# Second attention of a two-layer block: queries and output projection from rounded parts, fills dealt anew

## What is computed

```python
x = x + tanh(g_ffn[0]) * L0_ffn(...)                    # its sum is taken up in the second attention
x = x + tanh(g_xattn[1]) * L1_xattn(layernorm(x), ctx_768, ...)
x = x + tanh(g_ffn[1]) * L1_ffn(layernorm(x), ...)

def L1_xattn(x, y):                     # 16 heads of 32, 120 keys to a batch
    q = (x @ wq + bq).reshape(B, SQ, 16, 32)
    k = (y @ wk + bk).reshape(B, SKV, 16, 32)
    v = (y @ wv + bv).reshape(B, SKV, 16, 32)
    attn = softmax(einsum('bqhd,bkhd->bhqk', q, k) / sqrt(32))
    return einsum('bhqk,bkhd->bqhd', attn, v).reshape(B, SQ, 512) @ wo + bo
```

## Time and profile before

| | |
|---|---|
| median of 3 runs | 3941.38 us (3939.68 to 3944.68) |
| the profiled execution | 3940.56 us |
| its span in the trace | 3938.5 us |
| busy over the span | PE 94%, PEld 74%, DVE 74%, ACT 48%, POOL 28% |
| the second attention in the trace | about 2033 to 2557 us |
| the second mixture of experts | from there to the end, with TensorE's matmuls on nearly the whole chain that ended last |

### The profile page before, as it was taken

One profiled execution on the slowest core, in us unless ns is written; L12 is line 12 of the kernel. 1 busy time (PEld: TensorE's weight loads), 2 busy tenths in 40 slices (PEclk: granted clock), 3 DMA queues, 4 the chain that ended last, 5 costly groups with the idle time before them and its releaser, 6 DMA issues. The chain is left out here.

```text
span 3938.5 us, 62704 instructions
## 1 busy us (share of the span) xinstructions
PE 3699.6 (94%) x21884; PEld 2925.5 (74%) x21884; DVE 2924.7 (74%) x4545; ACT 1903.8 (48%) x2703; POOL 1098.4 (28%) x1008
## 2 busy tenths in 40 slices
PE   7899999999899999999979999849999999999998
PEld 4556665566468889889965555549999999999997
DVE  5567766676658788787737888578888788888885
ACT  2555555556445555554425445314444444444443
POOL 2222211222001111111026565313333434333332
PEclk9999999999899999999989999959999999999999
DMA  4010010100248787776640221126877777776874
GB/s 161 29 32 13 29 34 31 32 11 20 81 160 277 245 284 248 263 272 204 205 158 34 74 93 54 49 87 206 238 235 234 229 217 238 237 238 208 237 234 128
DMA packets 386958, 596.53 MB, mean 151 GB/s; under 512 B 26559, under 2 KB 192511, under 8 KB 386559
## 3 DMA queue, kind: packets, MB, share of 16 engines
q1 hardware_dynamic: 352575, 521.68, 39.7%
q0 software_dynamic: 24864, 58.54, 6.8%
q10 hardware_dynamic: 9368, 14.33, 1.0%
HBM read 535.36 MB, written 59.12 MB: 151 GB/s over the span
## 5 line engine op out<-in xcount | busy, mean ns | idle before, releaser
L1282 DVE TENSOR_TENSOR e_all<-e_all_raw,e_WH 128x2048 fp32r<-128x2048 f32 x240 | 545.5, 2289 | 36.5 <-ACT e_WH L1276 22.9
L1441 PE MATMUL bank<-e_xh,e_WH 128*128 128x256 f32 x1984 | 563.6, 284 | 9.5 <-issue 9.5
L1441 PE MATMUL bank<-e_xh,e_all 128*128 128x256 f32 x1984 | 562.5, 284 | 0.0
L1441 PE MATMUL bank<-e_xl,e_WH 128*128 128x256 f32 x1984 | 562.5, 284 | 0.0
L1276 ACT ACTIVATE e_WH<-e_all_raw 128x2048 fp32r<-128x2048 f32 x240 | 458.3, 1910 | 189.0 <-DMA e_all_raw<-in_w 188.8
L1494 PE MATMUL bank<-e_WH,e_hh 128*128 128x512 f32 x1192 | 473.7, 397 | 0.0
L1494 PE MATMUL bank<-e_WH,e_hl 128*128 128x512 f32 x1192 | 468.3, 393 | 0.0
L1441 PEld LDWEIGHTS bank<-e_xh,e_WH 128*128 128x128 f32 x1984 | 379.4, 191 | 14.7 <-issue 13.7
L1441 PEld LDWEIGHTS bank<-e_xl,e_WH 128*128 128x128 f32 x1984 | 379.4, 191 | 0.9
L1441 PEld LDWEIGHTS bank<-e_xh,e_all 128*128 128x128 f32 x1984 | 379.4, 191 | 0.0
L1517 ACT ACTIVATE e_sil<-bank 128x256 f32<-128x256 f32 x248 | 95.2, 384 | 367.0 <-PE bank L1441 362.3
(11 more groups left out here) (380 smaller groups left out, 9242.6 us busy)
## 6 DMA issues: line engine op xcount, KB each, us to landing
e_all_raw<-in_w SPq DMA_DIRECT2D x320, 512.0 KB, 5.0
f_wl_raw<-in_w SPq DMA_DIRECT2D x120, 1024.0 KB, 6.3
e_all_raw<-in_w SPq DMA_DIRECT2D x80, 1024.0 KB
e_rest_raw<-in_w SPq DMA_DIRECT2D x72, 1024.0 KB, 5.5
f_X<-in_x SPq DMA_DIRECT2D x32, 256.0 KB, 2.7
f_R<-in_x SPq DMA_DIRECT2D x32, 256.0 KB, 4.3
x<-f_R SPq DMA_DIRECT2D x32, 256.0 KB, 2.0
a_X<-x SPq DMA_DIRECT2D x32, 256.0 KB, 4.8
```

Source lines behind the costliest of these rows:

```text
L1282: dve.tensor_tensor(self.WL(p), self.raw(p), self.WH(p).bitcast(F32), ALU.subtract).then_inc(self.w_ready.sem, 1)
L1441: mm = nc.tensor.matmul(up[n % RING][:, q * ROWS:q * ROWS + ROWS], w, xx[:, c, :], start=(c == 0 and i == 0), stop=(c == DC - 1 and i == 2))
```

## The change

It computes `q` and `o` from rounded parts. Each operand is split in a high part (rounded to `fp32r`, a form of float32 whose matmuls show as one record each) and a low part (the rest, rounded too); a product is then high x high, high x low and low x high, so twelve matmuls stand in the place of eight records. ScalarE writes the high parts of `yt` and `pv`, and VectorE then reads the same PSUM bank again and writes the low parts (`low`): eight more VectorE operations to a batch, and the bank is free only after them. The weights are split once, ScalarE rounding and VectorE subtracting (`weights_high`, `weights_low`).

`o` is no longer emptied by ScalarE. VectorE reads it from PSUM in `result`, gates it and adds the residual in one instruction. Keys and values are loaded for one batch at a time, the keys by DMA straight into `kcur`, so that ScalarE copies none. The fills are dealt anew: both `pv` that were done in step 7 are now done in steps 0 and 1 of the next body, `yt` stands beside `o` in steps 3 to 6, and two fills of `q` stand in step 7.

```diff
-FILLS1 = ((("q", 2), ("nt", 3), ("r", 2)),
-          (("q", 3), ("yt", 0), ("r", 3)),
-          (("pv", 2), ("yt", 1), ("pv", 3), ("yt", 2)),
-          (("yt", 3), ("o", 0), ("q", 0)),
-          (("o", 1),),
-          (("o", 2), ("nt", 0)),
-          (("o", 3), ("nt", 1), ("r", 0)),
-          (("q", 1), ("pv", 0), ("pv", 1), ("nt", 2), ("r", 1)))
+FILLS1 = ((("q", 2), ("r", 1), ("pv", 0), ("nt", 3)),
+          (("pv", 1), ("r", 2)),
+          (("pv", 2), ("q", 3), ("pv", 3), ("r", 3)),
+          (("o", 0), ("yt", 0)),
+          (("o", 1), ("yt", 1)),
+          (("nt", 0), ("o", 2), ("yt", 2)),
+          (("nt", 1), ("o", 3), ("yt", 3)),
+          (("q", 0), ("r", 0), ("q", 1), ("nt", 2)))
...
-NORM1_AT = {3: (2, 0), 4: (2, 1), 1: (1, 2), 2: (1, 3)}
+NORM1_AT = {4: (2, 0), 5: (2, 1), 2: (1, 2), 3: (1, 3)}
...
+                def load_kv(i):
+                    if i >= 2:
+                        sp.wait_ge(s_done, STEPS1 * (i - 1))
+                    for r in range(4):
+                        p = slice(DH1 * r, DH1 * r + DH1)
+                        sp.dma_start(kcur[p, i % 2, :, r % 2, :], k.kT1[p, :, ORDER[i] * CL:ORDER[i] * CL + CL]).then_inc(k_in[i % 2], 16)
+                    if i >= 2:
+                        wait_filled(sp, i - 2, ("pv", 3))
+                    sp.dma_start(V[:, i % 2, :], k.V1[:, ORDER[i], :]).then_inc(v_in[i % 2], 16)
...
                     elif kind == "q":
-                        pe.wait_ge(wq_in, 32)
+                        pe.wait_ge(w_ready, 1)
...
-                            mm = nc.tensor.matmul(m, wq[:, c, a * P:a * P + P], xT[:, c, :], start=(c == 0), stop=(c == DC - 1))
+                            wh, wl = (by_rows(w)[:, c, a * P:a * P + P] for w in (wqh, wql))
+                            for j, (w, x) in enumerate(((wh, xTh), (wh, xTl), (wl, xTh))):
+                                mm = nc.tensor.matmul(m, w, x[:, c, :], start=(c == 0 and j == 0), stop=(c == DC - 1 and j == 2))
...
+                def weights_high(to, raw, there):
+                    act.wait_ge(*there)
+                    act.activation(to[:, :], raw[:, :], ACT.Copy).then_inc(w_high, 1)
...
+                weights_high(wqh, wq_raw, (wq_in, 48))
                 for n in bodies:
+                    if n == 0:
+                        weights_high(woh, wo_raw, (wo_in, 48))
...
+                    bk_, c_ = fill(i, f)
+                    dve.wait_ge(filled[bk_], c_)
+                    dve.wait_ge(r_biased, a)
+                    dve.scalar_tensor_tensor(x, mb[bk_], k.gate[:, 1:2], x, ALU.mult, ALU.add).then_inc(emptied[bk_], 1)
                     wait_emptied(dve, i, f)
-                    dve.wait_ge(r_biased, a)
-                    dve.tensor_tensor(x, x, gated[:, t % 2, :], ALU.add).then_inc(x3_ready, 1)
-                    dve.wait_ge(x3_ready, a)
                     dve.bn_stats(bst3[:, t, :], x).then_inc(bn3_step, 1)
...
+                def low(n, f):
...
+                    dve.wait_ge(kept_high, high(i, f))
+                    if kind == "yt":
+                        part = slice(a * P, a * P + P)
+                        x = dve.tensor_tensor(xTl[:, :, part], chunks(mb[bk_]), xTh[:, :, part].bitcast(F32), ALU.subtract)
+                    else:
+                        x = dve.scalar_tensor_tensor(OTl[:, a, :], mb[bk_], bv[:, a:a + 1], OTh[:, a, :].bitcast(F32),
+                                                     ALU.add, ALU.subtract)
+                    x.then_inc(emptied[bk_], 1)
...
+                weights_low(wql, wq_raw, wqh, 1)
                 for n in bodies:
                     for s in range(STEPS1):
                         u = STEPS1 * n + s
+                        if n == 0 and s == 0:
+                            weights_low(wol, wo_raw, woh, 2)
                         if softmax(n):
                             centre(u)
+                        low(n, FILLS1[s][0])
...
                             total(u)
-                        for f in FILLS1[s]:
+                        for j, f in enumerate(FILLS1[s]):
+                            if j:
+                                low(n, f)
```

More of the change, by code:

```diff
@@ L1696, in attention1 @@
         chunks = lambda bk_: bk_.rearrange("p (c n) -> p c n", c=DC)
-        wq_in, wo_in, kv_in, bf_in, folded, kzeroed = \
-            sem("wq_in"), sem("wo_in"), sem("kv_in"), sem("bf_in"), sem("folded"), sem("kzeroed")
-        k_ready = sem("k_ready")
+        wq_in, wo_in, bf_in, folded, kzeroed = sem("wq_in"), sem("wo_in"), sem("bf_in"), sem("folded"), sem("kzeroed")
+        k_in, v_in = [sem(f"k_in{i}") for i in range(2)], [sem(f"v_in{i}") for i in range(2)]
+        w_high, w_ready, kept_high = sem("w_high"), sem("w_ready"), sem("kept_high")
         x_in = [[sem(f"x_in{r}{t}") for t in range(QT)] for r in range(2)]
@@ L1738, in turned_in, with high @@
             return u if 0 <= u < STEPS1 * B else None
+        def high(i, f):
+            n = len(SPLIT1) * (i + LATE.get(f, 1) + 2) + SPLIT1.index(f)
+            return sum(1 for m in range(n + 1) if there(m // len(SPLIT1) - 2, SPLIT1[m % len(SPLIT1)]))
         comb = lambda i: i >= PLAIN
@@ L1900, in do @@
                         for c in range(DC):
-                            mm = nc.tensor.transpose(m[:, c * P:c * P + P], Y[:, a, c * P:c * P + P], k.ident[:, :])
+                            mm = nc.tensor.transpose(m[:, c * P:c * P + P], Y[:, (QT * i + a) % YRING, c * P:c * P + P], k.ident[:, :])
                     elif kind == "q":
-                        pe.wait_ge(wq_in, 32)
+                        pe.wait_ge(w_ready, 1)
                         for t in range(QT):
@@ L1917, in do @@
                         for c in range(DC):
-                            mm = nc.tensor.matmul(m, OT[:, c, a * P:a * P + P], wo[:, c, :], start=(c == 0), stop=(c == DC - 1))
+                            oh, ol = (o[:, c, a * P:a * P + P] for o in (OTh, OTl))
+                            for j, (o, w) in enumerate(((oh, woh), (oh, wol), (ol, woh))):
+                                mm = nc.tensor.matmul(m, o, by_rows(w)[:, c, :], start=(c == 0 and j == 0), stop=(c == DC - 1 and j == 2))
                     elif kind == "nt":
@@ L1943, in _ @@
             def _(act):
-                act.wait_ge(kzeroed, 1)
-                def keys(i):
-                    if i == 0:
-                        act.wait_ge(kv_in, 48)
-                    if i >= 2:
-                        act.wait_ge(s_done, STEPS1 * (i - 1))
-                    for r in range(4):
-                        p = slice(DH1 * r, DH1 * r + DH1)
-                        copy = act.activation(kcur[p, i % 2, :, r % 2, :], kT[p, :, ORDER[i] * CL:ORDER[i] * CL + CL], ACT.Copy)
-                    copy.then_inc(k_ready, 1)
+                def weights_high(to, raw, there):
+                    act.wait_ge(*there)
+                    act.activation(to[:, :], raw[:, :], ACT.Copy).then_inc(w_high, 1)
                 def keep_turned(u, i):
@@ L1967, in empty @@
                     kind, a = f
-                    if kind == "r" or not there(n, f):
+                    if kind in ("o", "r") or not there(n, f):
                         return
@@ L1974, in empty @@
                     if kind == "yt":
[L1975 removed]
+                        act.activation(xTh[:, :, a * P:a * P + P], chunks(m), ACT.Copy).then_inc(kept_high, 1)
+                        return
                     elif kind == "q":
[L1977 removed]
                         x = act.activation(qT[:, a, :], m, ACT.Identity, bias=bq[:, a:a + 1])
[L1979 to L1982 removed]
                     elif kind == "pv":
[L1985 removed]
+                        act.activation(OTh[:, a, :], m, ACT.Identity, bias=bv[:, a:a + 1]).then_inc(kept_high, 1)
+                        return
                     else:
@@ L2005, in _ @@
                             empty(n, f)
-                        if s == 5 and 0 <= n + 1 < B:
-                            keys(n + 1)
             @block.vector
@@ L2029, in norm @@
                     dve.wait_ge(rst, QT * i + t + 1)
-                    if i:
-                        wait_filled(dve, i - 1, ("yt", t))
-                    dve.tensor_scalar(Y[:, t, :], X[:, i % 4, t, :], mv[:, t, 0:1], rstd[:, t:t + 1], ALU.subtract, ALU.mult)\
+                    y = QT * i + t
+                    if y >= YRING:
+                        wait_filled(dve, (y - YRING) // QT, ("yt", (y - YRING) % QT))
+                    dve.tensor_scalar(Y[:, y % YRING, :], X[:, i % 4, t, :], mv[:, t, 0:1], rstd[:, t:t + 1], ALU.subtract, ALU.mult)\
                         .then_inc(y_ready, 1)
@@ L2076, in logits, with weights_low @@
                     dve.tensor_copy(k.logits[:, ORDER[i] * QT + t, :], mb[bk_][:, 0:E]).then_inc(emptied[bk_], 1)
+                def weights_low(to, raw, top, n):
+                    dve.wait_ge(w_high, n)
+                    dve.tensor_tensor(to[:, :], raw[:, :], top[:, :].bitcast(F32), ALU.subtract).then_inc(w_ready, 1)
```

(8 more changed lines are left out.)

55 lines of the change are left out of this document (28 added, 27 removed).

## The result

The changed kernel takes 3948.88 us (median of 20 runs, 3945.79 to 3952.67), the kernel before beside it 3940.89. The ratio is 1.0019, 95% interval 1.0013 to 1.0026: 8.0 us slower, where 7 us faster was forecast. The profiled execution took 3948.01 us, 7.5 more than the one of before; its span is 3946.2 us. The second attention ends 8.6 us later than before and what comes behind it is unchanged within 1 us, so the loss is in `attention1`.

The account below looks back on a forecast made before the run. VectorE was taken to pace the changed kernel, TensorE a close second. Start +9.5, batches 0 and 1 +1.0 and +0.1, batches 2 to 5 -12.5, batch 6 -0.5, batch 7 -2.6, tail -1.2: together -6.2, forecast 3934 us, range 3918 to 3952.

Parts of the forecast that it names:

- the last term of the sum: Tail of the second attention: four `o` of 2.80 us, serial with `result`, gain 1.2 us.
- The layout of steps 0 to 2: Start of a batch: TensorE waits for banks and low parts; VectorE works without a gap to 15.7 and 23.6 us.
- Start: Start of the second attention: weight splits and low parts make the first maximum 9.5 us late, at 2074.5.
- the layout by hand of both lists: One batch with expert sums on TensorE and VectorE: a cycle of 59.8 us; batches 2 to 5 gain 12.5 us.
- VectorE leading: Batches with expert sums: VectorE's list of 56.1 us exceeds TensorE's 49.7 and sets the pace; chance 0.63.
- TensorE a close second: Batches of the second attention: TensorE follows VectorE closely, with a list of 49.7 us against 56.1.
- idle some 10 us a batch: Batches 2 to 5: TensorE stands idle about 10 us in each, waiting for VectorE's low parts and `result`.
- The blocks of the earlier trace: Six residual sums of 3.87 to 4.21 us instead of 0.69 as GpSimd begins; expected to end with the PSUM read.
- (a): Batches 1 to 6: VectorE hides in gaps, TensorE paces at 52.1 us; kernel 3897, milder form 3920; chance together 0.12.
- (b): Norms of step 5: GpSimd blocks one for 3.5 us or more in batches 2 to 5; kernel 3956; chance 0.2.
- (c): Split fills no faster than priced, or 3.43 us again: step 7 lasts 1.3 us longer per batch; 3944; chance 0.05.
- The precision rule: Fills of `q` and `o`: four passes for FP32 would make three products 2.57 us; the forecast used 2.80.

Follow-up runs that it names:

- the four corners: Old deal plain, old deal split, new deal plain, new deal split, each with the sum from PSUM and keys by batch: 3931.25, 3977.57, 3925.51, 3948.88 us.

## Why the prediction was wrong, step by step

- **The step that failed is the last term of the sum,** "the tail, four `o` of 2.80 but serial with `result`, gains 1.2". It priced the tail by the length of fills that are in it before and after, and not by which fills the new deal leaves in it. The layout of steps 0 to 2 had the mechanism in so many words (`nt` needs the bank of `r`, which VectorE reads only after its `total`; `o` waits for the low part of the last `pv`), but was drawn for the cycle and not continued past the last softmax. There nothing else keeps TensorE busy. The first `o` comes 19.3 us after the last maximum (2535.59 less 2516.34) instead of 13.8, and from there to the last logits 31.5 pass instead of 26.1. Nor do the four `o` gain by themselves. Four of them, 0.63 shorter each, are 2.5 us, of which the prediction kept 1.2 without working it out. Measured, from the start of the first to that of the last 12.4 us pass before (2532.39 to 2544.75) and 15.4 after (2535.59 to 2550.97). The first ran at the lower clock and took 5.5 us (to 2541.09). The new deal also has `nt` in front of the third and the fourth, and it needs the bank that `result` of the `o` before has to free; before, the second and the third ran without a pause.
- **What it consists of:** four `pv` instead of two behind the last maximum, and `nt` behind the logits, both through the deal (51.4 in the plain kernel with the new deal, 37.5 with the old); the lower clock, which filled waits gave back 4.8 of; the bank held for the low part (1.5). These overlap: the 51.4 has a lower clock in it too. By the four corners the deal is the main part, since at the new deal the split leaves the tail 0.7 shorter.
- **Start:** +10.2 for +9.5, by the steps named; the early split of `wo` gave back 4.6, against 1.91 + 2.28 = 4.2.
- **Batches:** the layout by hand of both lists was right to 0.3 us in batches 2 to 5 (59.67 for 59.8) and to 0.6 in batches 1 and 6. Its reading, VectorE leading, is borne out by the runs without low parts and with only the queries split. For "TensorE a close second" there is the tie at the end of step 7, and no more: 12 us less of TensorE in 60 moved nothing, since the layout had left out that `nt` of step 7 waits for the logits. I said that TensorE would be idle some 10 us a batch; it is 7.2.
- **Sizes:** fills of 12 x 0.233 us, the sum at 711 ns, low parts at 657 and 749 for 690 and 750: right. The blocks of the earlier trace rows are gone from the sum, and all 32 ran in 752 ns or less. The Trainium skill (GPSIMD Engine Reference, Specifications) names GpSimd's contention with VectorE instructions of two SBUF inputs; the trace agrees, since the new sum reads only one operand from SBUF.
- **Rivals:** (a) would have left TensorE idle under 4 us; it did not come, and couldn't while VectorE has 54 us of work. (b), norms blocked by GpSimd, did not come either: no L2091 took over 1.34 us in the whole stage (one in each of batches 2 to 5 took 1.3, in step 7), and the batches with expert sums came out at 59.7. (c) did not come. The time landed between (c)'s 3944 and (b)'s 3956, but through a mechanism that I had not listed. That the range held it is luck: its upper part was there for (b). The forecast and the chances had the time on the other side.
- **The precision rule:** the Trainium skill (FP8 and Floating Point Precision, TensorE Precision Notes) has true FP32 as four passes. Three products as three quarters of that would be 2.57 us, an estimate; the fills took 2.80, as the row said, and the row holds.

## What to carry to other kernels

When work is dealt anew over the steps of a pipeline, lay out the last pass as well as the cycle: list what is left behind the last step, with the bank that each fill takes and who frees it. A faster form of the matmul must be charged with what it adds to the engine that paces the loop (here eight operations a batch and two splits at the start: 23 us more in all, where the products alone saved some 10 in the one run without low parts). Where two engines' paths end together, taking work from one of them need not show its share; look for the wait that takes its place. Changes that come bundled should be priced and tried one by one: three parts of this one were faster, and hid behind the fourth.

## What the runs showed of the hardware beyond that

- Less work made TensorE slower. With a third of the products its clock fell to 0.70 between 2342 and 2350 of that run, and batches grew by 1.3 us. In the tail, matmuls whose result nobody reads gave back 4.8 us in one kernel and 2.7 in another.
- With one operand in PSUM, 512 elements took VectorE no longer than with both in SBUF: 657 ns for a subtraction, against 691 in the earlier trace rows, and 711 for a gated sum, against 0.74 us in the earlier trace rows.
- The split of `wq` took 3.35 us instead of 2.28, begun while GpSimd ran two bias sums; like the sums of the earlier trace rows it reads two operands from SBUF. The forecast had taken that in (an end at 2053.3, measured 2053.4). A single case, not tried further:

```profile
2050.07 3.35 DVE L2102 TENSOR_TENSOR a_wql<-a_wql_raw,a_wqh 128x2048 fp32r<-128x2048 f32 x1
```
